# A one-hot comparison whose number row moves from SBUF to PSUM, beside a stage of gathers

## What is computed

```python
xn = _layernorm(x)
msgs = xn[src]                                            # E rows of 256
summed = segment_sum(msgs, dst, num_segments=N)
counts = segment_sum(ones(E), dst, num_segments=N)
agg = summed / maximum(counts, 1.0)[:, None]
gnn = relu(agg @ W_l.T + b_l + xn @ W_r.T) + xn
mix = linear attention over all nodes (8 heads)           # q, k, v from xn, then @ wo + bo
x = x + gnn + mix
x = x + layernorm(mixture of 8 experts, top 2, on layernorm(x))
```

## Time and profile before

| | |
|---|---|
| median of 3 runs | 2998.41 us (2996.05 to 2999.78) |
| the profiled execution | 2995.67 us, its span 2994.2 us |
| busy of the span | PE 67%, PEld 51%, DVE 52%, ACT 29%, POOL 57% |
| instructions | PE 10270, DVE 3558, ACT 2055, POOL 1705 |
| gathers | 1661, busy 1642.3 us |
| one-hot instructions | 391, busy 272.1 us |
| granted TensorE clock, mean | 0.808 of full speed |

### The profile page before, as it was taken

How to read it: one execution, slowest core, us unless ns; L and a number is a source line. 1 busy time by engine, 2 the same in 40 slices (tenths; PEclk the granted TensorE clock), 3 DMA queues, 4 the chain that set the end, 5 groups by cost and what they waited for, 6 DMA issues and landing times.

```text
span 2994.2 us, 36137 instructions
## 1 busy us (share of the span) xinstructions
PE 1998.9 (67%) x10270; PEld 1540.2 (51%) x10270; DVE 1566.0 (52%) x3558; ACT 867.3 (29%) x2055; POOL 1703.5 (57%) x1705
## 2 busy tenths in 40 slices
PE   7896565555555555556555556555565569999998
PEld 6774343344344334334434434433443469999997
DVE  7884544444444454444444445444444457777777
ACT  4552211211111121111121112111111145555564
POOL 2226777777777777777777777777777700000000
PEclk9997776777777777777677777777767789999999
DMA  5333443443444444344344344444434422212212
GB/s 153 114 113 100 123 121 115 123 123 112 123 123 115 119 121 118 115 122 122 112 123 123 111 122 123 119 116 122 122 112 123 116 66 78 69 63 74 73 63 66
DMA packets 192237, 326.99 MB, mean 109 GB/s; under 512 B 32703, under 2 KB 138216, under 8 KB 192200
## 3 DMA queue, kind: packets, MB, share of 16 engines
q0 software_dynamic: 80160, 219.14, 25.2%
q1 hardware_dynamic: 111624, 107.01, 11.4%
q10 hardware_dynamic: 416, 0.39, 0.1%
HBM read 275.21 MB, written 51.20 MB: 109 GB/s over the span
## 4 chain that ended last, share of the span: by engine, by line
POOL 51%; PE 20%; issue 17%; DVE 6%; DMA 2%; ACT 2%; POOLq 1%; ACTq 0%; DVEq 0%; SPq 0%
POOL ring L638 51%; PE pd L1116 9%; PE pa L1101 5%; PE pc L1101 4%; DMA ring<-xn_table,idxb 2%; DVE bst L1164 1%; ACT yT L651 1%; DVE yT L1202 1%; DVE nv L1186 1%; DMA yT<-in_x 1%; PE pa L1074 0%; PE pa L1075 0%; POOLq L634 0%; DVE yT L1208 0%; DVE nh L1190 0%
## 5 line engine op out<-in xcount | busy, mean ns | idle before, releaser
L638 POOL DMA_INDIRECT ring<-xn_table,idxb x1661 | 1642.3, 989 | 510.8 <-issue 500.4
L1074 PE MATMUL pa<-ring,ohh 128*128 128x256 f16 x1661 | 542.3, 340 | 907.1 <-DMA ring<-xn_table,idxb 832.0
L1074 PEld LDWEIGHTS pa<-ring,ohh 128*128 128x128 f16 x1661 | 194.3, 117 | 1090.5 <-issue 632.2
L1075 PE MATMUL pa<-ring,ohh 128*128 128x257 f16 x1661 | 552.4, 346 | 0.0
L1332 DVE TENSOR_TENSOR ring<-ring 64x514 f32<-64x514 f32 x49 | 33.8, 690 | 586.3 <-ACT ring L737 586.3
L737 ACT ACTIVATE ring<-pa 128x257 f32<-128x257 f32 x196 | 74.3, 379 | 917.9 <-PE pa L1075 917.2
L990 PE MATMUL pd<-mats,work 128*128 128x256 f32 x784 | 314.0, 544 | 0.9 <-DVE work L1349 0.9
L1116 PE MATMUL pd<-parts 128*128 128x256 f32 (+1 forms) x1568 | 312.3, 283 | 1.8 <-DVE parts L1516 1.8
L1323 DVE TENSOR_TENSOR ohh<-iota_f,edges 128x512 f16<-128x512 f32 (+1 forms) x391 | 272.1, 725 | 11.2 <-PE pa L1075 2.5
L1116 PEld LDWEIGHTS pd<-parts 128*128 128x128 f32 (+1 forms) x1568 | 253.4, 188 | 10.3 <-DVE parts L1516 2.4
L1075 PEld LDWEIGHTS pa<-ring,ohh 128*128 128x128 f16 x1661 | 197.1, 119 | 101.9 <-issue 42.9
(11 more groups left out here) (193 smaller groups left out, 3334.5 us busy)
## 6 DMA issues: line engine op xcount, KB each, us to landing
ring<-xn_table,idxb POOLq DMA_INDIRECT x1661, 2.8
yT<-in_x SPq DMA_DIRECT2D x24, 512.0 KB, 4.1
xn_table<-ring SPq DMA_DIRECT2D x24, 512.0 KB, 4.8
work<-in_x SPq DMA_DIRECT2D x48, 256.0 KB
x_rows<-work SPq DMA_DIRECT2D x48, 256.0 KB
y_rows<-work SPq DMA_DIRECT2D x48, 256.0 KB
work<-y_rows SPq DMA_DIRECT2D x24, 512.0 KB, 4.2
work<-x_rows SPq DMA_DIRECT2D x24, 512.0 KB, 3.9
```

The source lines that it names most:

```text
L638: pool.indirect_dma_start(out=msgs[:, k, 0:PARTS * D], out_offset=None, in_=xn_table[:, :], in_offset=bass.IndirectOffsetOnAxis(ap=idxb[:, ...
L1074: mm(pa[:, t % 2, 0:D], oh[:, slot, :], msgs[:, k, 0:D], start=begins, stop=False, skip_group_check=True)
L1075: ins = mm(pa[:, t % 2, 0:D + 1], oh[:, slot, :], msgs[:, k, D:2 * D + 1], start=False, stop=ends, skip_group_check=True)
```

## The change

The number row is copied once, ahead of the gather stage, from `iota_f` into bank 0 of `pc`, and every one-hot reads it there. A new semaphore, `iota_placed`, makes VectorE wait for its own copy. Three waits of VectorE (for the number row, the edge lists and the last statistics) now stand ahead of the memset of `msgs`' ones instead of behind it.

```diff
+            dve.wait_ge(s["iota_float"], 1)
+            dve.wait_ge(s["raw_taken"], 2 * NG)
+            dve.wait_ge(s["p1_stats"], NQ + 1)
             dve.wait_ge(s["xn_stored0"], quad_dmas(NQ, 0))
             dve.wait_ge(s["xn_stored1"], quad_dmas(NQ - 1, 1))
             V.memset(msgs[:, :, PARTS * D:SLOT], 1.0).then_inc(s["ones_set"], 1)
-            dve.wait_ge(s["iota_float"], 1)
-            dve.wait_ge(s["raw_taken"], 2 * NG)
-            dve.wait_ge(s["p1_stats"], NQ + 1)
+            V.tensor_copy(pc[:, 0, 0:WIN + STRIP], iota_f[:, :]).then_inc(s["iota_placed"], 1)
+            dve.wait_ge(s["iota_placed"], 1)
...
-                V.tensor_tensor(oh[:, slot:slot + m, :], bc(iota_f[:, c0:c0 + WIN], m), where, ALU.is_equal)\
+                V.tensor_tensor(oh[:, slot:slot + m, :], bc(pc[:, 0, c0:c0 + WIN], m), where, ALU.is_equal)\
                     .then_inc(s["oh_ready"], 1)
```

More of the change, by code:

```diff
@@ L237, in build_layer @@
         pd = ctx.enter_context(nc.psum_tensor("pd", [P, 4, 512], F32))
-        names = """waits_taken iota_set iota_float mask_step wk_loaded consts_set ident_set raw_padded raw_loaded raw_float raw_turned raw_taken
+        names = """waits_taken iota_set iota_float iota_placed mask_step wk_loaded consts_set ident_set raw_padded raw_loaded raw_float raw_turned raw_taken
             flag_a flag_sum flag_added flag_set w_loaded biases_loaded wlr_turned wlr_taken bias1_set
```

## The result

The changed kernel takes 2961.94 us (median of 4 runs, 2961.39 to 2968.4) against 2999.1 us (4 runs, 2996.05 to 3001.28), a ratio of 0.9882 with a 95% interval of 0.9867 to 0.9897. That is 37 us by the medians. The two profiled spans, whose parts can be added up, differ by 33.7 us (2994.2 and 2960.5). The forecast was 2966.4 us, range 2951 to 2981.

A forecast was written before the change was run, and what follows sets the result against it. POOL's 1661 back-to-back gathers were taken to bound the gather stage. Terms of -31.6 us (gathers caught by one-hots) and 0 for the rest, rounded to -32 us, gave 2966.4 us, range 2951 to 2981.

The forecast's parts named there:

- The catch by one-hots: Gather stage: 113 gathers made long by beginning inside a one-hot lose their time over 0.944 us, -31.6 us.
- the check from the other side: One-hots' 54% share of busy time among two-SBUF-input instructions, applied to the 74.3 us of gather excess: 40 us.
- as if: Gather stage: a caught gather behaves as if needing its indices 0.12 us after it began and unable to have them.
- The catch by others: Gather stage: seven other VectorE lines keep two SBUF inputs; their catch is drawn afresh, 40 against 40.6 us, counted as 0.
- even-phase estimate: Seven other lines' catch if gather starts fell evenly over the 1.25 us period: 36.7 us.
- The bounds of 25 and 55: Limits in us for the seven other lines' catch after the change, giving total times of 2981 and 2951 us.
- The one-hot's duration and the COPY: VectorE: one-hots stay at 0.69 and 0.83 us; the new copy and its wait take 0.4 us, hidden; both 0 us.
- The cover: Start of gather stage: TensorE catches up and waits for gathers at 271.52 us, hiding the copy; 0.4 us without it.
- The first: One-hots: the move frees nothing, gathers stay at 989 ns and the time at 2998 us; chance 0.04.
- The third: One-hots: slow broadcast reads from PSUM make VectorE the bound, 3390 us at 4 us more each; chance 0.01.
- The second: Additions of lines 1374 to 1391: their phase to the gathers locks badly, so others catch more, 3016 us; chance 0.03.
- fourth: Other catching lines: their catch falls to 17 us, so much more is won, 2943 us; chance 0.04.

The follow-up runs named there:

- the extra additions: One more VectorE addition of two SBUF rows ahead of each one-hot, against the changed kernel: 2975.56 us with output in SBUF, 2976.02 us with output in PSUM.
- the extra copy: One more VectorE float32 copy of 512 columns from SBUF to SBUF ahead of each one-hot, against the changed kernel: 2972.34 us.

## Why the prediction was right

**What bounds.** POOL's gathers, back to back. The stage shortened by the 33.7 us that the gathers lost, with an idle time equal to the tenth. The opening says that the engines meet only at semaphores; VectorE and GpSimd meet here without one, in a way that depends on where VectorE's inputs lie.

**The catch by one-hots, -31.6 us.** Gone entirely: 142 starts inside, none long. Counting pairs was right, and the check from the other side (40 us by busy time) would have been 8 too many. That one-hots stand in trains of two or three, as the extra additions do, fits this, but no run shows that it is the whole reason. What in the gather is held, the reading of its indices or another step, no run tells either: the prediction's "as if" stays one.

**The catch by others, 40.6 to 40.** It came out at 38.4 us. The even-phase estimate of 36.7 hit here, and the forecast's 40 with it; that is luck rather than a rule: it leaves out that a catch moves the next gathers, and it overstates the one-hots before (0.116 us for 294 and, by the same formula, 0.186 for the 97 long ones make 52; 31.6 measured) and the extra additions more than threefold. The bounds of 25 and 55 held it and all the redraws of the experiments with seven lines (33.4 beside the extra copy to 41.5).

**What of it is in the time.** 31.6 and 2.2 us from the two counts are all of the difference of the spans, 33.7. The medians differ by 37; the rest is within the scatter of the runs, which spread over 5 us before and 7 after.

**The one-hot's duration and the COPY.** 684 for 689 ns. The copy took 0.34 us (I had put it and its wait at 0.4), and TensorE waited 3.00 us for the first one-hot instead of 2.55; by 272.25 us it waited for gathers again. The cover held.

**The rivals.** The first, that the move frees nothing, falls by the count of 142 and by the run that takes back the row alone. The third falls with 684 ns. The second and fourth didn't come about here; the run with the bias in PSUM shows that the second's mechanism is real and of the size of a few us. The inference of the Trainium skill's page "SBUF — State Buffer", section "Who interferes with whom", that an addition of two SBUF tensors doesn't stall descriptor generation, would have left these gathers alone; the extra addition holds 80 of them for 12.7 us. Whether it is the descriptor generation that waits or a step before it, the runs don't show.

## What to carry to other kernels

Where GpSimd issues small indirect transfers back to back and is the bound, compare the mean of one with its median, and lay the long ones beside VectorE's instructions: what exceeds the median may be waiting for an instruction that reads two SBUF tensors, or for a fast copy from SBUF to SBUF. Moving one operand, the one that never changes first of all, into an unused PSUM bank cost nothing per instruction here and took that wait away. Price it by counting the caught transfers, not by an even phase, and expect the rest to be redrawn by some us with each edit, so that the last lines moved may give nothing.

## What the runs showed of the hardware that I had not expected

- A float32 copy of 512 columns from SBUF to SBUF holds gathers with a single input (82 for 11.4 us), at 0.42 us a copy, and touches them a second time about 0.46 us into the gather (48 of 48). A reciprocal with a single SBUF input holds none (0 of 122).
- The direction of the output makes no difference for additions: 12.6 us caught with the output in PSUM, 12.7 with it in SBUF.
- A held gather spares following ones: with the same program but for one operand's memory, 81 gathers start inside an instruction's window where it can hold them, and 160 where it can't.
